# The first attention's residual addition moves from VectorE to accumulating transfers, its statistics to the gate's product and ScalarE

## The reference, cut to what matters

```
x = x + gnn0(layernorm(x), adj)      # attention over a graph's nodes, then elu
x = x + ffn0(layernorm(x))           # 8 experts, top-1 gate, capacity 2560 rows each
x = x + gnn1(layernorm(x), adj)      # a second attention
x = x + ffn1(layernorm(x), edges)    # edge gate over 524288 edges, 4 experts, top 2
```

## Time and profile before

| | |
|---|---|
| median of 3 runs | 3020.04 us (3017.76 to 3021.19) |
| the profiled execution | 3023.74 us, its span 3021.7 us |
| busy | PE 1764.9 us, DVE 2256.2 us, ACT 1154.4 us, POOL 1878.8 us |
| mean granted TensorE clock | 0.794 of full speed |

### The profile page before, as it was taken

One profiled execution on the slowest core, in us unless ns is written; L12 is line 12 of the kernel. 1 busy time (PEld: TensorE's weight loads), 2 busy tenths in 40 slices (PEclk: granted clock), 3 DMA queues, 4 the chain that ended last, 5 costly groups with the idle time before them and its releaser, 6 DMA issues. The chain is left out here.

```text
span 3021.7 us, 31014 instructions
## 1 busy us (share of the span) xinstructions
PE 1764.9 (58%) x8786; PEld 1213.8 (40%) x8831; DVE 2256.2 (75%) x4431; ACT 1154.4 (38%) x2319; POOL 1878.8 (62%) x1723
## 2 busy tenths in 40 slices
PE   0777773048788885476853356545655565456545
PEld 0566653035565553365752233222322232233223
DVE  7999999889999999897733665565556655665566
ACT  2676773234444443266841222222322232223222
POOL 4702244845444555477777777777777777777771
PEclk9898885579999998688956677777777776777777
DMA  5698000101111111222121122212221222122211
GB/s 218 207 353 332 18 22 14 34 29 41 31 48 32 54 37 35 77 60 67 38 52 30 31 43 45 43 31 43 45 43 31 43 45 43 31 43 45 43 31 36
DMA packets 170129, 192.34 MB, mean 64 GB/s; under 512 B 59241, under 2 KB 126096, under 8 KB 169008
## 3 DMA queue, kind: packets, MB, share of 16 engines
q1 hardware_dynamic: 107616, 118.69, 11.8%
q0 software_dynamic: 57088, 62.48, 10.3%
q10 hardware_dynamic: 5328, 9.97, 0.9%
HBM read 91.70 MB, written 105.25 MB: 65 GB/s over the span
## 5 line engine op out<-in xcount | busy, mean ns | idle before, releaser
L1578 POOL DMA_INDIRECT sort_ping<-node_table,sort_ping x1024 | 996.3, 973 | 312.0 <-issue 293.7
L1213 POOL DMA_INDIRECT token_results<-arena,token_of x160 | 257.6, 1610 | 290.0 <-ACT arena L1147 213.8
L636 DVE TENSOR_TENSOR sort_ping<-sort_pong 128x1024 f32<-128x1024 f32 (+1 forms) x232 | 394.9, 1743 | 6.9 <-ACT sort_pong L1083 2.3
L636 DVE TENSOR_TENSOR sort_pong<-sort_ping 128x1024 f32<-128x1024 f32 (+1 forms) x230 | 390.3, 1738 | 11.2 <-ACT sort_ping L1083 6.7
L1716 PE MATMUL x_b_featT<-ident,x_feat 128*128 128x128 f32 x128 | 34.8, 427 | 603.5 <-PEq L1310 603.5
L1206 POOL DMA_INDIRECT slots<-arena,send x128 | 196.8, 1538 | 304.0 <-ACT arena L1105 270.4
L1460 DVE TENSOR_TENSOR win_score<-win,masked 128x320 f32<-128x320 f32 x64 | 28.7, 489 | 424.7 <-DMA win<-edge_table,win_ids 423.5
L1722 PE MATMUL x_b_hid<-x_featT,x_w 128*128 128x512 f32 x512 | 310.0, 759 | 28.3 <-PEq L1310 28.3
L1729 PEld LDWEIGHTS x_b_res<-x_w,x_hid 128*128 128x128 f32 x2048 | 242.1, 194 | 97.3 <-issue 97.3
L1716 PEld LDWEIGHTS x_b_featT<-ident,x_feat 128*128 128x128 f32 x128 | 22.9, 216 | 608.8 <-issue 608.8
L1729 PE MATMUL x_b_res<-x_w,x_hid 128*128 128x128 f32 x2048 | 266.8, 284 | 0.0
(11 more groups left out here) (367 smaller groups left out, 4040.6 us busy)
## 6 DMA issues: line engine op xcount, KB each, us to landing
edge_table<-zeros SPq DMA_DIRECT2D x8, 5120.0 KB, 35.7
sort_ping<-node_table,sort_ping POOLq DMA_INDIRECT x1024, 2.4
arena<-slots SPq DMA_DIRECT2D x40, 260.0 KB, 2.6
slots<-zeros SPq DMA_DIRECT2D x2, 5120.0 KB, 24.4
edge_table<-sort_ping SPq DMA_DIRECT2D x64, 160.0 KB, 1.8
out_dram<-x_y ACTq DMA_DIRECT2D x33, 256.0 KB
x<-in_x_dram SPq DMA_DIRECT2D x4, 2048.0 KB, 16.4
adjacent<-in_adj_dram SPq DMA_DIRECT2D x32, 256.0 KB, 2.7
```

The source lines that it names most:

```text
L636: step(dve.tensor_tensor(vb[:, :, t, :], va[:, :, 0, :], va[:, :, 1, :], op))
L1213: pool.indirect_dma_start(rows_dram, bass.IndirectOffsetOnAxis(token_of[:, n % 4, r:r + 1], 0), res[:, n % 2, r, :], None, bounds_check=TO ...
L1578: pool.indirect_dma_start(rows[:, u, c, :], None, table_dram, bass.IndirectOffsetOnAxis(ids[:, u, c:c + 1], 0)).then_inc(rows_in[u], 16)
```

## The change

The elu is written into `grown` itself, and VectorE stops there for the group. GpSimd issues one transfer per group, SBUF to SBUF, 128 partitions by 512 numbers, which adds `grown` to x and raises `updated` by 16. From group 4 on `grown` has two buffers, the second in the memory of the adjacency blocks. The gate's weight gets a ninth column of -1/128, so the gate's product brings minus the row's mean; ScalarE squares x plus that number and sums it (`act_square`, four instructions a group), which gives the variance. The last group of each eight still uses bn_stats. The norm's steps stand later, `choose` stands behind `dve_scores`, and GpSimd's scatters are interleaved with the accumulating transfers.

```diff
+class SumNorm:
...
+    def dve_before_root(self, dve):
+        s, t = self.scratch, self.stats
+        last = t[:, -PER:, :]
+        spread, sq = s[:, 0, 0:PER], s[:, 0, PER:2 * PER]
+        dve.tensor_tensor(spread, last[:, :, 1], last[:, :, 4], ALU.subtract).then_inc(self.made, 1)
...
+        dve.tensor_tensor(last[:, :, 0], sq, last[:, :, 5], ALU.add).then_inc(self.made, 1)
+        dve.wait_ge(self.made, self.steps + 4)
+        dve.wait_ge(self.squares, (self.turn + 1) * (t.shape[1] // PER - 1))
+        dve.tensor_scalar(s[:, 2, :], t[:, :, 0], 1.0 / FEAT, EPS, ALU.mult, ALU.add).then_inc(self.made, 1)
+
+    def act_root(self, act):
+        act.wait_ge(self.made, self.steps + 5)
+        act.activation(self.scratch[:, 1, :], self.scratch[:, 2, :], ACT.Sqrt).then_inc(self.rooted, 1)
+
+    def dve_behind_root(self, dve):
+        dve.wait_ge(self.rooted, self.turn + 1)
+        dve.reciprocal(self.rstd[:, :], self.scratch[:, 1, :]).then_inc(self.made, 1)
+        dve.wait_ge(self.made, self.steps + 6)
+        dve.tensor_tensor(self.shift[:, :], self.mean, self.rstd[:, :], ALU.mult).then_inc(self.done, 1)
...
             if live(m):
                 act.wait_ge(self.under_s, m + 1)
-                ge(act, self.updated, m)
-                act.activation(self.grown[:, :, :], self.under[:, :, :], ACT.Exp, scale=-1.0).then_inc(self.grown_s, 1)
+                ge(act, self.updated, 16 * (m if m < 5 else m - 1))
+                act.activation(self.grown_of(m)[:, :, :], self.under[:, :, :], ACT.Exp, scale=-1.0).then_inc(self.grown_s, 1)
...
+    def grown_of(self, m):
+        return self.growns[m % 2 if m >= 4 else 0]
+
+    def pool_update(self, pool, m):
+        if not live(m):
+            return
+        pool.wait_ge(self.elu, m + 1)
+        ge(pool, self.updated, 16 * m)
+        pool.dma_start(self.x[:, m * PER:(m + 1) * PER, :], self.grown_of(m)[:, :, :], accum_op=ALU.add).then_inc(self.updated, 16)
...
             dve.wait_ge(self.grown_s, m + 1)
-            dve.scalar_tensor_tensor(self.out[:, :, :], self.grown[:, :, :], -1.0, self.out[:, :, :], ALU.add, ALU.max).then_inc(self.elu, 1)
-            dve.wait_ge(self.elu, m + 1)
-            dve.tensor_tensor(mine, mine, self.out[:, :, :], ALU.add).then_inc(self.updated, 1)
+            grown = self.grown_of(m)
+            dve.scalar_tensor_tensor(grown[:, :, :], grown[:, :, :], -1.0, self.out[:, :, :], ALU.add, ALU.max).then_inc(self.elu, 1)
+            return
...
     def pe_turn(self, pe, g):
-        pe.wait_ge(self.updated, g + 1)
+        pe.wait_ge(self.updated, 16 * (g + 1))
...
+    def act_square(self, act, g):
+        act.wait_ge(self.kept, g + 1)
+        ge(act, self.squares, g - g // self.chunk)
+        for v in range(PER):
+            q = g * PER + v
+            last = act.activation(self.squared[:, v, :], self.x[:, q, :], ACT.Square, bias=self.into[:, g % self.chunk * PER + v, EXPERTS:EXPERTS + 1],
+                                  accum_out=self.stats[:, q, 0:1])
+        last.then_inc(self.squares, 1)
...
+            dve.memset(gate_w[:, EXPERTS:EXPERTS + 1], -1.0 / FEAT).then_inc(gate_centred, 1)
             for n in range(-2, LAST_OF[-1] + 3):
...
-                if n - 1 in LAST_OF:
-                    choose(LAST_OF.index(n - 1))
                 att0.dve_held(dve, n - 1)
                 att0.dve_scores(dve, n + 2)
+                if n - 1 in LAST_OF:
+                    x0_norms[LAST_OF.index(n - 1)].dve_behind_root(dve)
+                    choose(LAST_OF.index(n - 1))
...
                 att0.dve_updated(dve, n - 1)
-                if n >= GATED and n % GATED == 0 and n <= GROUPS:
-                    dve.wait_ge(att0.stats_s, n)
-                    x0_norms[n // GATED - 1].dve_before_root(dve)
-                if n > GATED and n % GATED == 1 and n <= GROUPS + 1:
-                    x0_norms[n // GATED - 1].dve_behind_root(dve)
+                if n in LAST_OF:
+                    last = (LAST_OF.index(n) + 1) * GATED - 1
+                    dve.wait_ge(att0.updated, 16 * (last + 1))
+                    bn(dve, stats, x, last).then_inc(att0.stats_s, 1)
+                    dve.wait_ge(att0.stats_s, LAST_OF.index(n) + 1)
+                    x0_norms[LAST_OF.index(n)].dve_before_root(dve)
...
                 att0.act_step_first(act, n, n % 4)
-                if n > GATED and n % GATED == 1 and n <= GROUPS + 1:
-                    x0_norms[n // GATED - 1].act_root(act)
+                if n - 1 in PROJECTED and PROJECTED[n - 1] % GATED != GATED - 1:
+                    gate.act_square(act, PROJECTED[n - 1])
+                if n in LAST_OF:
+                    x0_norms[LAST_OF.index(n)].act_root(act)
...
+            for n in range(LAST_OF[-1] + 3):
+                att0.pool_update(pool, n)
+                for c in range(CHUNKS):
+                    if 2 < n - LAST_OF[c] <= 2 + GATED:
+                        scatter(c * GATED + n - LAST_OF[c] - 3)
+            for g in range(GROUPS - GATED, GROUPS):
+                scatter(g)
```

More of the change, by code:

```diff
@@ L136, in dve_behind_root, with __init__ @@
         dve.scalar_tensor_tensor(self.shift[:, :], s[:, 0, :], -0.5, self.rstd[:, :], ALU.mult, ALU.mult).then_inc(self.done, 1)
+class SumNorm:
+    def __init__(self, sem, stats, mean, scratch, rstd, shift, squares, before=None):
+        if before is None:
+            self.made, self.rooted, self.done = (sem(f"norm_{n}_x0") for n in ("step", "root", "done"))
+        else:
+            self.made, self.rooted, self.done = before.made, before.rooted, before.done
+        self.turn = 0 if before is None else before.turn + 1
+        self.steps = 6 * self.turn
+        self.stats, self.mean, self.scratch, self.rstd, self.shift, self.squares = stats, mean, scratch, rstd, shift, squares
+    def dve_before_root(self, dve):
[3 more added lines that the diff above has]
+        dve.tensor_tensor(spread, last[:, :, 1], last[:, :, 4], ALU.subtract).then_inc(self.made, 1)
+        dve.wait_ge(self.made, self.steps + 1)
+        dve.scalar_tensor_tensor(sq, spread, 0.25 * FEAT, spread, ALU.mult, ALU.mult).then_inc(self.made, 1)
+        dve.wait_ge(self.made, self.steps + 2)
+        dve.tensor_tensor(sq, sq, last[:, :, 2], ALU.add).then_inc(self.made, 1)
+        dve.wait_ge(self.made, self.steps + 3)
+        dve.tensor_tensor(last[:, :, 0], sq, last[:, :, 5], ALU.add).then_inc(self.made, 1)
[10 more added lines that the diff above has]
+        dve.tensor_tensor(self.shift[:, :], self.mean, self.rstd[:, :], ALU.mult).then_inc(self.done, 1)
 class Attention:
@@ L170, in __init__ @@
         self.masked_s = masked_s
+        self.growns = [self.grown, self.grown]
     def act_step(self, act, n, u):
@@ L367, with __init__ @@
 class Gate:
-    def __init__(self, sem, x, updated, chunk, ident, weight, featT, b_featT, b_out, into):
+    def __init__(self, sem, x, updated, chunk, ident, weight, featT, b_featT, b_out, into, stats, squared):
+        self.stats, self.squared, self.squares = stats, squared, sem("gate_squares")
         self.turned, self.featT_s, self.projected, self.kept = (sem(f"gate_{n}") for n in ("turned", "featT", "projected", "kept"))
@@ L483, in front @@
                          view, att_small, banks, masked_s, key_made)
+        att0.growns[1] = adjacent[:, 1, :].bitcast(F32).rearrange("p (v i) -> p v i", v=PER)
         GATED, LEVELS = 8, LOG_EDGES - LOG_COLS
@@ L491, in front @@
         LAST_OF = [LEAD + (c + 1) * GATED - 1 + c for c in range(CHUNKS)]
[L492 to L495, removed]
         spare = adjacent[:, :, :].rearrange("p c f -> p (c f)").bitcast(F32)
@@ L514, in front @@
         gate = Gate(sem, x, att0.updated, GATED, ident, gate_w[:, :], of(spare, 1024, PER, NODES),
-                    banks[:, 4, :].rearrange("p (v i) -> p v i", v=PER), banks[:, 1, 0:PER * EXPERTS].rearrange("p (v e) -> p v e", v=PER), logits)
+                    banks[:, 4, :].rearrange("p (v i) -> p v i", v=PER), banks[:, 1, 0:PER * (EXPERTS + 1)].rearrange("p (v e) -> p v e", v=PER), logits,
+                    stats, of(spare, 0, PER, FEAT))
+        x0_norms = []
+        for c in range(CHUNKS):
+            cols = slice(c * ROWS, (c + 1) * ROWS)
+            x0_norms.append(SumNorm(sem, stats[:, cols, :], logits[:, :, EXPERTS], scratch[:, :, cols], rstd[:, cols], shift[:, cols], gate.squares,
+                                    x0_norms[-1] if c else None))
         route, less, exped, chosen_s, ranked, placed, ordered, routed = (sem(f"route_{n}") for n in (
@@ L584, in front @@
                  att0.below_s, att0.exped, att0.probs_turned, att0.probsT_s, att0.out_s, att0.shared, att0.held, att0.under_s, att0.grown_s, att0.elu,
-                 att0.updated, att0.stats_s, gate.turned, gate.featT_s, gate.projected, gate.kept, route, less, exped, chosen_s, ranked, placed, ordered, routed,
```

(12 more changed lines are left out.)

9 lines of the change are left out of this document (4 added, 5 removed).

## The result

The changed kernel takes 3028.55 us as a median of 14 runs (3024.64 to 3032.37); the kernel before, timed beside it in 14 runs, 3021.26 us (3017.76 to 3024.11). The ratio is 1.0024, 95% interval 1.0016 to 1.0032: 7.3 us slower. I had forecast 3012 us. The profiled execution took 3032.37 us, 8.6 us above that of before. VectorE's first return from TensorE comes at 664.67 us against 656.25, 8.4 us later: the whole loss lies ahead of it.

What follows compares the result with a forecast made beforehand. VectorE looked like the loop's bound, but a ScalarE and TensorE chain holds single-step turns to 9.2 to 9.8 us. The terms +6 - 1 - 4 - 11 + 2 = -8 us gave 3012 us, range 3005 to 3019.

Steps and rivals of the forecast that it cites:

- Landing: Accumulating transfer beside SyncE's clears, first half of the loop: lands in 8.7 us, bounds 3.1 to 11.6 us.
- Start-up and single-step turns 5 to 9: Groups 0 to 4 lose 6 us waiting for landings with one buffer; turns 5 to 9 gain 1 us.
- 0.8 us for the squares in ScalarE's round: Part of the start-up's +6 us: the squares join ScalarE's round and add 0.8 us.
- The new wait of TensorE's gate transposes is covered up to a landing of about 8 us: In the loop, gate transposes come nearly a turn behind the elu, so landings up to about 8 us cost nothing.
- third rival: Landing of 11.6 us beside the clears delays early groups and turns 5 to 9: +11 us, 3031 us; chance 0.15.
- -4 us of turns 10 to 12: Choice of experts moves behind the scores and fills the wait: four fifths of 3 x 1.52 us gained.
- ScalarE's two send buffers come free about 0.5 us too late in six pairs: 3: Turns 13 to 28: scatters stand behind additions released a turn later, giving back 3 us.
- other terms of turns 13 to 28: VectorE sheds 24.3 us; given back: score waits 6.8, square root 2 x 1.1, last groups' bn_stats twice 0.8.
- Squares: ScalarE's four squares with sums per group take 1.4 us, bounds 1.27 to 2.4, free within the chain.
- fourth rival: Squares take 2.4 us and lengthen ScalarE's round in single-step turns and pairs: 3022 us; chance 0.12.
- Tail: Behind the loop, group 16's scatter is about 10 us late, mostly regained by faster issues: +2 us (0 to +8).
- fifth rival: The scatters behind the loop don't catch up: +8 instead of +2 us, 3018 us; chance 0.10.

Runs made afterwards that it cites:

- e4: Changed kernel with VectorE adding groups 0 to 13 and transfers adding only from group 14 on: 3009.18 us, 0.9957 of before.
- e6: Changed kernel with SyncE's clears of token_results and the edge tables held back until the elu of group 31: 3041.89 us, 1.0061 of before.
- e5: Changed kernel with two buffers of `grown` from the start instead of from group 4: 3026.45 us, 1.0009 of before.
- e2: Changed kernel without transfers: VectorE adds all groups, squares stay on ScalarE: 3002.52 us, 0.9937 of before.
- e1: Changed kernel with GpSimd's scatter placed ahead of the same turn's accumulating transfer: 3007.70 us, 0.9949 of before.
- e8: Changed kernel with VectorE adding groups 0 to 13, transfers after that, and scatters ahead of the transfers: 2997.63 us, 0.9908 of before.
- e9: Changed kernel without transfers or squares: VectorE adds and takes bn_stats of all groups, new order of norm and `choose` stays: 3017.57 us, 0.9983 of before.

## Why the prediction was wrong

*Landing, held.* 8.7 us was estimated beside the clears, 8.2 and 8.4 measured, and 3.4 behind them. The Trainium skill's rule ("DMA: Bandwidth & Descriptors", section "Anatomy of one DMA — SWDGE (gpsimd) path") gives 2.6 us for these 256 KB (estimate). Without the clears a copy took 2.3 and an addition 3.4 us, so the rule is near; beside the clears it is not.

*Start-up and single-step turns 5 to 9, right to turn 9 by luck.* Turn 2 ended at 138.90 instead of 136.32, 2.6 us late where I had 3.5; turn 9 started at 201.92 instead of 195.95, 6.0 us behind, at the end of the 4 to 6 us forecast. But this was the sum of two errors. The gain was larger (without transfers in these turns, e4, turn 9 starts at 189.98, 6.0 us ahead of before), and so was the loss, 11.9 us. The 0.8 us for the squares in ScalarE's round had no row behind it: in e4 turns 4 to 8, squares included, last 8.9 to 9.2 us.

*"The new wait of TensorE's gate transposes is covered up to a landing of about 8 us" failed.* The landing was just past that limit: TensorE, ready 1.97 us earlier, could go on at 211.85 only, with the addition that GpSimd had begun to issue at 201.99. So the third rival's mechanism was there at 8.2 us already; its point of decision, "about 10 us", was too high. The -4 us of turns 10 to 12 were eaten by it: from the start of turn 9 to that of turn 13 the changed kernel took 56.85 us, before 56.29, and e6, with a landing of 3.3 us, 53.02. Turn 13 started 6.5 us behind instead of 1 behind, and the transfers' price by then was 14.2 us where the start-up term had 6. By e6 8.7 us of these are the clears', by e5 3.3 us the single buffer's; no run has both, so how far the two overlap is open.

*"ScalarE's two send buffers come free about 0.5 us too late in six pairs: 3" failed, the larger step.* It was 14.9 us of waits, and undoing the order alone gave turns 13 to 28 12.5 us. I had seen that the scatter stands behind an addition that VectorE releases a turn later, but put what this costs the buffers at 0.5 us in six pairs, with no row to size it. The buffers have two turns in all: a scatter that starts 13 us late and takes 8 us to issue ends when ScalarE wants its buffer again. The first wait, 7.07 us, also had a scatter that landed beside the last clears: SyncE was issuing clears of the edge table until 269.46 + 27.66 = 297.1 us, before until 276.6. With the clears moved away (e6) the first wait is 2.27 us, and turns 13 to 28 take 197.35 us, so a part of this loss too is the clears'.

*The other terms of turns 13 to 28 were right in their sum.* With the order undone they took 190.83 us, 14.1 less than before; the forecast without its 3 us for the buffers was 14. No run takes them one by one. VectorE's own single-step turn is 8 us, as said.

*Squares, held.* Four take 1.55 us (307.24 to 308.79) against 1.4, each with a separate write of 0.20 us of which some 0.1 us shows. The fourth rival falls with e2.

*Tail, right in its sum.* +2 was taken, +2.6 measured, but again of two parts: e1 shows a gain of 4.3 us against before, and the order of GpSimd's queue costs 6.9 us. Group 16's scatter started at 509.70, 17 us later than before, and the last one 7.5 us later, not 4 to 12 us earlier, because the loop was not ahead. The fifth rival's mechanism was there; that an undisturbed tail would gain was not seen. One reading behind this term was too wide: the issue of 0.97 us at 634.05 doesn't show a resting VectorE, which was in a 128x1024 step of the sort then; only the one at 534.86, in a wait of VectorE, does. VectorE's wait for the experts' first transposes stayed, 6.23 us.

What stays open: the tail's gain of 4 to 5 us goes with the squares, since where no scatter is late it takes 171.5 to 172.6 us with them (e1, e2, e8) and 176.03 without (e9), but through which instructions isn't shown; why the squares bring nothing beside the transfers as built; and how far the single buffer and the gate transposes share the loss of the first groups.

## What to carry to other kernels

When work moves to a queue that issues in order, look at what stands behind it there: an instruction that waits for a late producer delays everything that was ready, and a ring of two buffers turns that into a stall of the engine that fills it. A transfer's landing is to be costed by what else is in flight where it runs; the same addition took 3.4 us and 8.2 us. When a change has two parts, time each alone and with the other: here the squares were worth 13 us alone and nothing beside the transfers, the transfers cost 14 us alone and 26 beside the squares, and the whole looked like a small loss.

## What was not expected of the hardware

An accumulating transfer of 256 KB within SBUF landed 1.1 us later than a copy of the same bytes (3.4 against 2.3 us), 1.4 us beside the clears. The 13 additions beside them also slowed the clears: a 5 MB clear took 39.0 us in place of 35.7 at the median (35.9 in e2, which has no additions).
